# A window-attention and stencil kernel: the projection from two rounded parts of y, transfers issued by double step, the last strips' stencils first in their block

## The reference, cut to what matters

```python
# layer 0, on h = _gn(x): windows of 8x8 = 64 tokens, 6 heads of 32 channels
o = irfft2(rfft2(q) * rfft2(k))              # circular convolution of q and k per channel
attn = softmax(einsum('bhnd,bhmd->bhnm', o, v) + bias)
y = einsum('bhnm,bhmd->bhnd', attn, v)       # back to image order
x1 = x + einsum('bchw,oc->bohw', y, proj_w) + proj_b
# layer 1, on g = _gn(x1)
out = x1 + merge_w @ (g + laplacian(g)) + merge_b
```

## Time and profile before

| | us |
|---|---|
| median of 3 runs | 5852.0 (5837.02 to 5854.65) |
| the profiled execution, its time | 5841.05 |
| the profiled execution, its span | 5839.3 |
| PE busy | 5608.1 (96%) |
| DVE busy | 4152.6 (71%) |
| ACT busy | 3394.7 (58%) |
| POOL busy | 3368.2 (58%) |

### The profile page before, as it was taken

How to read it: one execution, slowest core, us unless ns; L and a number is a source line. 1 busy time by engine, 2 the same in 40 slices (tenths; PEclk the granted TensorE clock), 3 DMA queues, 4 the chain that set the end, 5 groups by cost and what they waited for, 6 DMA issues and landing times.

```text
span 5839.3 us, 207528 instructions
## 1 busy us (share of the span) xinstructions
PE 5608.1 (96%) x91644; PEld 4730.3 (81%) x91644; DVE 4152.6 (71%) x7166; ACT 3394.7 (58%) x6629; POOL 3368.2 (58%) x2494
## 2 busy tenths in 40 slices
PE   7999999999999999999999999999999999999977
PEld 5888888888888888888888888888888888888854
DVE  5777677776777777777777767777677777677743
ACT  3666665565655656556565566556665566655532
POOL 1333356666666666566666666666666666666653
PEclk9999999999999999999999999999999999999998
DMA  4222123333333333333333323333333332232344
GB/s 134 71 63 60 56 77 101 107 87 88 108 105 102 84 97 101 106 101 83 98 108 107 97 79 109 105 104 96 86 104 110 98 89 78 79 90 72 87 112 131
DMA packets 392498, 550.52 MB, mean 94 GB/s; under 512 B 24822, under 2 KB 284601, under 8 KB 391610
## 3 DMA queue, kind: packets, MB, share of 16 engines
q1 hardware_dynamic: 391612, 537.24, 32.7%
HBM read 335.82 MB, written 201.33 MB: 92 GB/s over the span
## 4 chain that ended last, share of the span: by engine, by line
PE 82%; ACT 13%; issue 2%; DVE 2%; POOL 0%; SPq 0%; DMA 0%; POOLq 0%; ACTq 0%
PE b_q L551 23%; PE b_t L653 8%; PE b_s L671 8%; PE b_q L639 7%; PE b_t L629 6%; PE b_s L499 4%; PE b_s L501 4%; ACT probsT L949 3%; PE b_s L561 3%; ACT probs L1091 3%; PE b_s L558 3%; PE b_t L611 3%; PE b_s L512 2%; ACT qkh L949 2%; PE b_s L510 2%
## 5 line engine op out<-in xcount | busy, mean ns | idle before, releaser
L1216 POOL TENSOR_TENSOR probs<-probs,srec 128x768 f32<-128x768 f32 x512 | 880.6, 1720 | 1604.2 <-DVE srec L932 1604.2
L1202 POOL TENSOR_TENSOR probs<-probs,smax 128x768 f32<-128x768 f32 x512 | 754.3, 1473 | 583.6 <-DVE smax L892 582.8
L887 DVE TENSOR_TENSOR probs<-b_s,posb 128x768 f32<-128x768 f32 x512 | 490.5, 958 | 815.0 <-PE b_s L671 815.0
L949 ACT ACTIVATE vs<-b_q 128x192 f32<-128x192 f32 x1024 | 338.4, 330 | 1240.0 <-PE b_q L551 1239.9
L881 DVE TENSOR_TENSOR qkl<-b_q,qkh 128x384 fp32r<-128x384 f32 x1024 | 571.0, 558 | 628.4 <-ACT qkh L949 594.5
L551 PE MATMUL b_q<-wnh,xh 128*128 128x288 f32 x2048 | 708.1, 346 | 38.6 <-DVE qkl L881 33.5
L551 PE MATMUL b_q<-wnl,xhl 128*128 128x288 f32 x2048 | 611.8, 299 | 1.2 <-issue 1.2
L551 PE MATMUL b_q<-wnh,xhb 128*128 128x288 f32 x2048 | 608.4, 297 | 2.3 <-issue 2.3
L551 PE MATMUL b_q<-wnl,xh 128*128 128x288 f32 x2048 | 608.6, 297 | 0.0
L551 PE MATMUL b_q<-wnh,xl 128*128 128x288 f32 x2048 | 607.5, 297 | 0.7 <-issue 0.7
L1133 POOL TENSOR_TENSOR dg<-late 128x645 f32<-128x645 f32 x352 | 561.9, 1596 | 75.9 <-DMA late<-x_dram 51.1
(11 more groups left out here) (184 smaller groups left out, 13742.3 us busy)
## 6 DMA issues: line engine op xcount, KB each, us to landing
ld<-in_x SPq DMA_DIRECT2D x192, 512.0 KB, 4.8
late<-x_dram SPq DMA_DIRECT2D x112, 640.0 KB, 5.0
xs<-in_x SPq DMA_DIRECT2D x128, 512.0 KB, 5.4
x_dram<-late SPq DMA_DIRECT2D x128, 512.0 KB, 3.1
out<-late SPq DMA_DIRECT2D x128, 512.0 KB, 2.9
late<-x_dram SPq DMA_DIRECT2D x240, 192.0 KB, 5.6
xs<-in_x SPq DMA_DIRECT2D x128, 256.0 KB, 5.8
x_dram<-late SPq DMA_DIRECT2D x128, 256.0 KB, 3.8
```

The costliest lines, as they stand in the source:

```text
L887: V.tensor_tensor(scored(i).rearrange("p (t q) m -> p t q m", q=4), scores.rearrange("p (t q m) -> p t q m", q=4, m=N), posb[:, :, :].unsq ...
L949: return A.activation(o, i, ACT.Copy)
L1202: P.tensor_tensor(probs[:, i % 2, :, :], probs[:, i % 2, :, :], smax[:, i % 2, :].unsqueeze(2).broadcast_to([128, 12, N]), ALU.subtract).t ...
L1216: P.tensor_tensor(probs[:, i % 2, :, :], probs[:, i % 2, :, :], srec[:, i % 2, :].unsqueeze(2).broadcast_to([128, 12, N]), ALU.mult).then_ ...
```

## The change

The projection takes y in two rounded parts. The y products of heads 4 and 5 now land on partitions 0 to 63 for both windows, so `yT` holds four column blocks, and ScalarE copies all 512 columns. At the end of the double ScalarE makes from it, in image order, `yh` (channels 0 to 127, rounded) and the lower half of `yb` (channels 128 to 191, rounded). GpSimd subtracts: `yl` is the remainder of the first, the upper half of `yb` that of the second. `project` makes each half of the output with five float32r products of 128 rows by 256 columns, against weights rounded once at the start (`wph`, `wpl`). VectorE adds them in two instructions. The weight and `fwd` are loaded to a place in `late` that is used later on for other things.

SyncE waits for the first v product of a double before it issues that double's share of transfers. In the last 16 strips all three units of a stencil go to the first double of the block. From `ALONE` on, pieces take the two PSUM regions by turns, and a piece waits for the last reader of its own region. GpSimd's sub goes ahead of the diagonal sum in a double.

```diff
-            rest = yT[:, 2, :, :].rearrange("p w (r c) -> p r w c", c=WS)
-            def project_a():
-                o = b_r[:, 0:256]
-                mm(o, wp[:, 0, :], yT[:, 0:2, :, :].rearrange("p i w (r c) -> p r (i w) c", c=WS),
-                   start=True, stop=False)
-                for i in range(2):
-                    mm(o.rearrange("p (r i w c) -> p i r w c", r=WS, i=2, w=2)[:, i], wp[:, 2 + i, :], rest,
-                       start=False, stop=(i == 1))
-            def project_b():
-                o = b_r[:, 256:384]
-                for i in range(2):
-                    out_rows = slice(i * CB, (i + 1) * CB)
-                    mm(o[out_rows], wp[:, 1, out_rows], yT[:, i, :, :].rearrange("p w (r c) -> p r w c", c=WS),
-                       start=True, stop=False, skip_group_check=True)
-                mm(o, wp[:, 4, :], rest, start=False, stop=True, skip_group_check=True).then_inc(proj_mm, 1)
+            def project(o, lo, n):
+                up = lo + 128
+                high, low, both = (t[:, :, :, :].rearrange("p r w c -> p (r w c)") for t in (yh, yl, yb))
+                mm(o, wph[:, 0, lo:up], high, start=True, stop=False)
+                mm(o, wpl[:, 0, lo:up], high, start=False, stop=False)
+                pe.wait_ge(yl_done, 2 * n)
+                mm(o, wpl[:, 1, lo:up], both, start=False, stop=False)
+                mm(o, wph[:, 1, lo:up], both, start=False, stop=False)
+                return mm(o, wph[:, 0, lo:up], low, start=False, stop=True)
...
-                    pe.wait_ge(yT_out, pair(4)[1])
+                    n = pair(4)[1]
+                    pe.wait_ge(yh_out, n)
...
-                    project_a()
+                    project(b_r[:, 0:256], 0, n)
...
-                    project_b()
+                    project(b_r[:, 256:512], CB, pair(4)[1]).then_inc(proj_mm, 1)
...
-                                q, c = (h * HD, i * N) if h < 4 else (i * N + (h - 4) * HD, 2 * N)
+                                q, c = (h * HD, i * N) if h < 4 else ((h - 4) * HD, (2 + i) * N)
...
+                if pair(3):
+                    act.wait_ge(yT_out, pair(3)[1])
+                    copy(yh[:, :, :, :], y_a)
+                    copy(yb[0:CB, :, :, :], y_b[0:CB]).then_inc(yh_out, 1)
...
+                if pair(3):
+                    pool.wait_ge(yh_out, pair(3)[1])
+                    P.tensor_tensor(yl[:, :, :, :], y_a, yh[:, :, :, :].bitcast(F32), ALU.subtract).then_inc(yl_done, 1)
+                    pool.wait_ge(yl_done, 2 * pair(3)[1] - 1)
+                    P.tensor_tensor(yb[CB:128, :, :, :], y_b[0:CB], yb[0:CB, :, :, :].bitcast(F32),
+                                    ALU.subtract).then_inc(yl_done, 1)
+                    pool.wait_ge(yl_done, 2 * pair(3)[1])
...
+            def double_started(j):
+                if j < DOUBLES:
+                    sp.wait_ge(v_mm, 2 * j + 1)
             for blk in range(BLOCKS + 1):
+                img, c = divmod(blk + 1, NS)
+                more_stats = 2 * c < NL and img + 1 < B
+                double_started(4 * blk)
+                if 2 <= blk <= STRIPS + 1:
+                    x1_store(blk - 2)
+                if more_stats:
+                    stat_load((img + 1) * NL + 2 * c)
+                double_started(4 * blk + 1)
+                u = 2 if blk == 0 else blk + 1
+                if u > 2 and u < STRIPS or blk == 0:
+                    strip_load(u)
+                double_started(4 * blk + 2)
                 v = blk - MERGE_LAG - 1
                 if 0 <= v < STRIPS:
-                    if blk < BLOCKS:
-                        sp.wait_ge(m_mm, m_count[8 * blk + 1])
                     result_store(v)
+                if more_stats:
+                    stat_load((img + 1) * NL + 2 * c + 1)
+                double_started(4 * blk + 3)
                 v = blk - STENCIL_LAG + 1
                 if 0 <= v < STRIPS:
-                    sp.wait_ge(m_mm, m_count[8 * blk + 3])
                     source_load(v)
...
-                if 1 <= blk <= STRIPS:
-                    x1_store(blk - 1)
-                if blk + 2 < STRIPS:
-                    strip_load(blk + 2)
...
+        def beside_q(it):
+            task = m_task(it)
+            return it >= ALONE and task is not None and task[0] == "piece" and task[2] % 2 == 1
...
+        def region_free(eng, it):
+            last = it - 1
+            while last > -5 and (m_task(last) is None or beside_q(last) != beside_q(it)):
+                last -= 1
+            m_wait(eng, last)
...
-                unit = stencil_unit(j - 1)
-                if unit and by_vector(*unit):
-                    late_stencil(*unit)
+                if late_strip(j) is not None:
+                    late_stencil(late_strip(j), 0)
+                    late_stencil(late_strip(j), 2)
...
+                if late_strip(j) is not None:
+                    for unit in range(3):
+                        centre(late_strip(j), unit)
                 a_result(2 * j)
...
-                if unit:
-                    diagonal(*unit)
-                    neighbours(*unit, 0)
                 if pair(2):
                     i, n = pair(2)
                     pool.wait_ge(max_done, n)
...
+                if unit:
+                    diagonal(*unit)
+                    neighbours(*unit, 0)
...
+                if late_strip(j) is not None:
+                    diagonal(late_strip(j), 1)
+                    neighbours(late_strip(j), 1, 0)
+                    neighbours(late_strip(j), 1, 1)
```

More of the change, by code:

```diff
@@ L120, in proj_blocks @@
     t = weight.T
[L121 to L124, removed]
+    return np.concatenate([t[:CA], np.concatenate([t[CA:], t[CA:]])], axis=1)
 def program(nc, x, out, w):
@@ L154, in program @@
         wnh, wnl = sb("wnh", [128, 2, 2, QKV], F32R), sb("wnl", [128, 2, 2, QKV], F32R)
-        wp, wm, mn = sb("wp", [128, 5, 128]), sb("wm", [128, 5, 128]), sb("mn", [128, 2, 5, 128])
+        wm, mn = sb("wm", [128, 5, 128]), sb("mn", [128, 2, 5, 128])
+        wph, wpl = sb("wph", [128, 2, C], F32R), sb("wpl", [128, 2, C], F32R)
         qkvb, biasrow = sb("qkvb_row", [1, QKV]), sb("biasrow", [128, QKV // 2])
@@ L171, in program @@
         vs, vT = sb("vs", [128, 8, C]), sb("vT", [128, 2, 3, 128])
-        osb, yT = sb("osb", [128, 6, N]), sb("yT", [128, 3, 2, N])
+        osb, yT = sb("osb", [128, 6, N]), sb("yT", [128, 4, 2, N])
+        yh, yl, yb = (sb(name, [128, WS, 4, WS], F32R) for name in ("yh", "yl", "yb"))
+        y_a, y_b = (yT[:, 2 * k:2 * k + 2, :, :].rearrange("p i w (r c) -> p r (i w) c", c=WS) for k in range(2))
         qkh, qkl = sb("qkh", [128, 2, QK], F32R), sb("qkl", [128, 2, QK], F32R)
@@ L198, in program @@
         mw1, mb2 = late[0:2, at + 16:at + 16 + HID], late[0:1, at + 16 + HID:at + 16 + HID + N * NH]
+        at += 16 + HID + N * NH
+        wp = late[:, at:at + 2 * C].rearrange("p (k n) -> p k n", k=2)
+        fwd = late[:, at + 2 * C:at + 2 * C + NF]
         b_q, b_t, b_s = ps("b_q", 2), ps("b_t", 4), ps("b_s", 2)
@@ L228, in program @@
         xh_done, xl_done, xhl_done = map(sem, ("xh_done", "xl_done", "xhl_done"))
-        sub_done, norm_done = map(sem, ("sub_done", "norm_done"))
+        sub_done, norm_done, yh_out, yl_done = map(sem, ("sub_done", "norm_done", "yh_out", "yl_done"))
         border_w, five_done, diag_done, nb_done, z_done, late_diag, late_nb, late_z = map(sem, (
@@ L297, in stencil_unit, with late_strip @@
             v = blk - STENCIL_LAG
-            return (v, ph // 2) if 0 <= v < STRIPS and ph < 6 else None
+            return (v, ph // 2) if 0 <= v < LATE and ph < 6 else None
         LATE = STRIPS - NS
-        def by_vector(v, unit):
-            return v >= LATE and unit != 1
+        def late_strip(j):
+            blk, ph = divmod(2 * j, 8)
+            v = blk - STENCIL_LAG
+            return v if LATE <= v < STRIPS and ph == 0 else None
         def pool_units(v, unit):
@@ L522, in m_slot @@
                 kind, at, p = task
-                m_wait(pe, it - 2 if it > ALONE and it % 4 in (1, 2) else it - 1)
+                region_free(pe, it)
                 if pair(2):
@@ L774, in _ @@
             dve.wait_ge(const_in, 16 * len(loads))
-            V.tensor_copy(fwdh[:, :], fwd[:, :])
+            V.tensor_copy(fwdh[:, :], fwd)
+            link(V.tensor_copy(wph[:, :, :], wp))
+            V.tensor_tensor(wpl[:, 0, :], wp[:, 0, :], wph[:, 0, :].bitcast(F32), ALU.subtract)
+            V.tensor_tensor(wpl[0:CB, 1, :], wp[0:CB, 1, :], wph[0:CB, 1, :].bitcast(F32), ALU.subtract)
+            V.tensor_scalar(wpl[CB:128, 1, :], ones[CB:128, 0:1].broadcast_to([CB, C]), 0.0, None, ALU.mult)
             group_parts(0)
@@ L919, in _ @@
                     dve.wait_ge(proj_mm, n)
-                    for t, m, at, width, src in ((0, CA, col, 32, b_r[:, 0:256]), (1, CB, col, 16, b_r[0:CB, 256:384]),
-                                                 (1, CB, col + 16, 16, b_r[CB:128, 256:384])):
```

(12 more changed lines are left out.)

15 lines of the change are left out of this document (5 added, 10 removed).

## The result

The changed kernel takes 5576.98 us (median of 4 runs, 5573.17 to 5581.64) where the kernel before took 5847.65 beside it: a ratio of 0.9539, 95% interval 0.9521 to 0.9557. That is 271 us, 85 more than the sum forecast. The profiled run took 5581.64 us with a span of 5579.7.

The account below looks back on a forecast made before the run. TensorE was taken to bound the kernel (82% of the chain, ScalarE 13%). Terms -170 + 44 - 65 + 5 = -186 from 5841 gave 5655, set at 5660 us; own range 5595 to 5725, 8 in 10 5585 to 5790.

Parts of the forecast that it names:

- projection with stalls and drain: Blocks 19 to 127: shorter projection products, -170 us; GpSimd's lateness, +44; small passes and exposed remainders, +5.
- last strips: Last 16 strips: stencils run beside the pieces, a strip falls from 13.28 to 8.6 us; -65 us, bounds 30 and 85.
- SyncE's transfers: Same transfers, held back until a double has begun: 0 on the path; TensorE's issue waits 0, within 30 us either way.
- Other: Four small VectorE passes before the loop and three exposed remainders at its end: together some 5 us added.
- the range's low end of 5595: Whole kernel: no stall, 75 us from the last strips and some issue waits gone give 5595 us.
- the figure chosen: GpSimd's and ScalarE's added work in the doubles: stalls of 0.1 us a double, 0.4 a block, 44 us.
- The port: VectorE and GpSimd share one port pair: 0.62 us back in each odd double, about 55 us more, 5715.
- the prediction's 10.0 us: GpSimd's work with the remainders in a double of phases 2 and 6, against a double of 9.7 us.
- slower rival: GpSimd's remainders cost 1.29 us each, 2.7 a pair, delaying yl in every double: 370 us lost, 6150; chance 0.12.
- first rival: GpSimd eats the projection's gain, by remainders of about 1.1 us or the port; only last strips gain: 5780; chance 0.17.
- third rival: Last strips: the source's transfers set the pace, a strip stays near 12 us, time 5700; chance 0.06.
- the fourth: Transfers at the starts of doubles delay a strip or TensorE's stream and give everything back: 5840; chance 0.03.

Follow-up runs that it names:

- new SyncE order alone: Kernel before with only SyncE's new order and waits: 5751.4 us, ratio 0.9844 to the kernel before.
- old last strips: Changed kernel with the stencils, regions and piece waits of before in the last 16 strips: 5632.0 us.
- the run with the old one: Changed kernel with SyncE's order and waits of before; projection and last strips stay changed: 5715.5 us, ratio 0.9779 to the kernel before.
- the run on the place inside the double: Changed kernel with SyncE's transfer groups of phases 0, 4 and 6 let go some 4 us later in the double: 5754.7 us.
- the deferred pass: Changed kernel with GpSimd's second neighbour pass of phase 2 moved behind the subtraction of phase 4: 5545.8 us.
- the border-first run: Changed kernel with ScalarE's border copies of a last strip put ahead of its three centres: 5567.6 us, ratio 0.9526 to the kernel before.

## Why the prediction was off, step by step

| term | forecast | measured | from |
|---|---|---|---|
| projection with stalls and drain | -170 + 44 + 5 = -121 | -119 | new SyncE order alone, against old last strips |
| last strips | -65 | -55 | old last strips, against the changed kernel |
| SyncE's transfers | 0, within 30 | -96 | kernel before, against new SyncE order alone |
| sum | -186 | -270 | |

("Other" of the prediction, 5, stands with the projection.) The three rows are steps of one way from the old kernel to the new, so their sum is the whole by construction. Taken in another order they differ: some 25 us of the end's 55 need the new SyncE order, as the run with the old one shows.

**The step that failed** is the one on SyncE's transfers: "So 0 on the path", and for the waits on issue, "Fewer transfers together might take some away, others may meet; I take 0, within 30 either way." The strip loads are indeed not on the path. But the waits of the earlier trace rows nearly all went (59 us on all lines to 1, with the new order alone), and a part of them had a second price that the earlier trace rows don't show: TensorE's clock at 1.2 GHz behind the stop, some 35 us in all. The rows were read, and for the right engine; the bound of 30 was set with no row, though the earlier trace rows alone had 50 us in it, the range's low end of 5595 had room for some 11 of them (5660 - 44 - 10 = 5606), and TensorE's granted clock was not looked at around one of these stops. The reason given, fewer transfers together, was not the one that decides either: it is when in a double they are in flight (the run on the place inside the double).

**The projection.** The main part was right in its pieces: 0.59 a half, remainders 0.73, ScalarE's copies covered. Phases 0 and 2 gained 0.48 and 0.28 (0.49 and 0.29 forecast), phases 4 and 6 0.21 and 0.17, so 0.40 a block is lost to stalls, the figure chosen. That the total fits is partly luck: it was thought of as 0.1 in every double, and phases 0 and 2 lose nothing. In phase 4 its place is yl, as the prediction had it: GpSimd's pass out of phase 2 makes it late, and the deferred pass takes it away. What holds phase 6 back by 0.12 stays open. In the drain "some 5 us" was too little, 13 by two runs. Between these two runs blocks 19 to 127 gained 125 for 126 forecast, and the blocks ahead of them 7 for 0, which makes up for the drain: that -119 comes so near to -121 is luck in this part.

**The port.** GpSimd's last pass over probs takes 1.92 us in the odd double shown, with VectorE's pass over two SBUF operands (xhl) beside it at 1.53. In the next odd double that pass takes 0.70, and GpSimd's second neighbour pass beside it takes 1.64 for its usual 1.18. The odd double, VectorE's pass and then GpSimd's:

```profile
2536.01 1.53 DVE L957 TENSOR_TENSOR xhl<-xs,xhl 64x512 fp32r<-64x512 f32 x1
```

```profile
2536.95 1.92 POOL L1246 TENSOR_TENSOR probs<-probs,srec 128x768 f32<-128x768 f32 x1
2538.83 0.74 POOL L1251 TENSOR_TENSOR yl<-yT,yh 128x256 fp32r<-128x256 f32 x1
2539.65 0.72 POOL L1253 TENSOR_TENSOR yb<-yT,yb 64x256 fp32r<-64x256 f32 x1
2540.45 1.48 POOL L1225 TENSOR_TENSOR probs<-probs,smax 128x768 f32<-128x768 f32 x1
```

That the two hold each other up agrees with the rule of the Trainium skill ("SBUF — State Buffer", section Terms). But it was so before: the kernel before has the same in each odd double, 1.97 us for the 1.47 that the prediction took for this pass.

```profile
2528.79 1.97 POOL L1216 TENSOR_TENSOR probs<-probs,srec 128x768 f32<-128x768 f32 x1 [2.11 <-DVE srec L932]
```

So GpSimd did have some 0.46 more to do in each odd double than the prediction's 10.0 us, where the prediction put 0.62 by the rule, and the stalls of 0.40 a block hold whatever that costs; 55 us on top of them did not come. How much of the 0.40 is the port's no run shows. The slower rival had its condition, a pair of remainders of 2.7 us, refuted by the 1.5 us pair; of the first rival's two conditions the remainders of 1.1 us did not come, the port's did, without eating the main part.

**The last strips.** The loop over the source's transfers was right: 8.85 a strip for 8.6. Two runs price it at 55, the stretches behind the last scores at 273.8 - 216.8 = 57. What is short of 65 fits the first strips of the last image, which take up to 17.3, the first of them at a granted clock of 0.50; about 10 of it was ScalarE's border behind the centres, which the border-first run took away. The prediction did not see that the loop also needs the new SyncE order: with the old one strips take 10.7. The third rival (12 us a strip) fell, and the fourth too: the transfers took nothing back.

## What to carry to other kernels

A wait on "issue" on the engine that sets the time is work to be had, not noise: look at what the DMA queues do in the microseconds ahead of it and at the granted clock behind it, and price both. Place transfers so that they have landed before TensorE's next instructions are due, here some 6.5 us into a double, ahead of the many short products; cutting one into small pieces keeps it in flight for longer. And when a queue is near full, as GpSimd's in phases 2 and 6, look for the one operation whose result is needed a double later and move that.

## What the hardware showed that was not expected

TensorE's instructions come through a DMA queue while the kernel runs, 16 KB for 256 of them, about one packet for every 7.5 us, and share the DMA engines with the kernel's transfers. 576 KB in 1168 packets, in flight until 7.8 us into a double, held them up; 576 KB in 144 packets, through at 6.7, did not; 4096-byte packets that kept the engines full from 5 to 7.5 us did. TensorE went on 1.1 to 1.6 us after such a packet had landed. Behind the stop of 2.56 us the granted clock was 0.50 for about 7 us. Whether the packet of instructions waits its turn for all that time, or is asked for late, no run here shows: the Trainium skill ("DMA: Bandwidth & Descriptors", section Queues, rings and completion order) says that a DMA engine takes turns between its queues packet by packet, and whether a delay of 1 to 3 us agrees with that can't be told from these traces.
